# One graph layer and a top-2 mixture of experts on one core: the last four row tiles reordered, three residual sums moved from VectorE to TensorE

## The reference, cut to what matters

```
def _L0_gnn_ref(x, edge_index, W1, b1, W2, b2):        # 2500 nodes, 512 features, 80000 edges
    agg = jax.ops.segment_sum(x[src], dst, num_segments=N_NODES)
    h = jax.nn.relu((x + agg) @ W1 + b1)
    return h @ W2 + b2

def _L0_ffn_ref(x, Wg, W1, b1, W2, b2):                # 8 experts, top 2, hidden size 256
    gate = softmax(xt @ Wg);  topv, topi = top_k(gate, 2);  topv = topv / (sum(topv) + 1e-6)
    out = sum over e of (gelu(xt @ W1[e] + b1[e]) @ W2[e] + b2[e]) * scores[:, e:e+1]

x = x + _L0_gnn_ref(_layernorm(x), edge_index, ...)    # called x2 below
x = x + _L0_ffn_ref(_layernorm(x), ...)                # the second layer norm gives xt
```

## Time and profile before

| | |
|---|---|
| median of 3 runs | 658.34 us (656.91 to 659.75) |
| profiled execution, its own time | 657.24 us |
| its span in the profile | 655.5 us |
| mean granted TensorE clock | 0.946 of full speed |
| graph sums end | 412.4 us from the span's start |
| first matmul of the expert stage | 458.75 us |
| first rows added to the output | 467.98 us |
| TensorE busy | 555.8 us, 85% of the span |
| VectorE, ScalarE, GpSimd busy | 413.9, 316.7, 251.2 us |

### The profile page before, as it was taken

How to read it: one execution, slowest core, us unless ns; L and a number is a source line. 1 busy time by engine, 2 the same in 40 slices (tenths; PEclk the granted TensorE clock), 3 DMA queues, 4 the chain that set the end, 5 groups by cost and what they waited for, 6 DMA issues and landing times.

```text
span 655.5 us, 10719 instructions
## 1 busy us (share of the span) xinstructions
PE 555.8 (85%) x3842; PEld 435.9 (67%) x3843; DVE 413.9 (63%) x805; ACT 316.7 (48%) x579; POOL 251.2 (38%) x219
## 2 busy tenths in 40 slices
PE   4776877799999999999999999925999999999900
PEld 2666767656756766766666665725989998889800
DVE  5866574687369777976986131589566664554541
ACT  2573766533252125124322300558776766777671
POOL 4450222203016005100700331025567877778763
PEclk9997899999899999999999999965999999999955
DMA  8160600020020310211122113779688989899995
GB/s 259 54 161 1 192 1 1 1 75 1 1 64 2 95 48 12 84 48 49 49 77 65 39 58 96 262 236 304 139 172 183 186 167 193 187 205 198 165 185 76
DMA packets 40302, 71.91 MB, mean 110 GB/s; under 512 B 10313, under 2 KB 14545, under 8 KB 39714
## 3 DMA queue, kind: packets, MB, share of 16 engines
q0 software_dynamic: 12704, 29.22, 22.6%
q1 hardware_dynamic: 26257, 37.34, 19.3%
q10 hardware_dynamic: 1288, 4.66, 2.4%
HBM read 46.07 MB, written 26.69 MB: 111 GB/s over the span
## 4 chain that ended last, share of the span: by engine, by line
PE 50%; DMA 13%; DVE 12%; POOL 10%; ACT 7%; issue 6%; SPq 1%; ACTq 0%; POOLq 0%; DVEq 0%
PE psum L1414 26%; PE psum L1398 9%; PE psum L1451 7%; POOL out_x L601 6%; DMA out_x<-y,target_i 6%; PE psum L1330 3%; POOL xg L594 3%; DVE hot_key L1047 2%; DMA slot_rows<-edge_pairs,start_i 2%; DVE hot_lo L1047 2%; DMA xg<-xt_d,token_i 2%; DMA b_now<-in_L_ffn_b 2%; DVE xT_rest L891 1%; DVE stat L861 1%; ACT y L823 1%
## 5 line engine op out<-in xcount | busy, mean ns | idle before, releaser
L663 ACT ACTIVATE counts<-psum 128x400 bf16<-128x400 f32 x125 | 62.6, 504 | 163.2 <-PE psum L1398 162.9
L1047 DVE TENSOR_TENSOR hot_key<-iota_key,key_w 128x1200 f16<-128x1200 f16 x125 | 105.7, 845 | 47.3 <-PE psum L1398 47.3
L1414 PE MATMUL psum<-counts,z_hi 125*128 125x500 bf16 x400 | 101.8, 375 | 1.6 <-ACT h L687 1.6
L601 POOL DMA_INDIRECT out_x<-y,target_i x54 | 88.5, 1639 | 36.3 <-SPq L480 15.0
L1414 PE MATMUL psum<-counts,z_lo 125*128 125x500 bf16 x400 | 101.5, 377 | 0.0
L1398 PE MATMUL psum<-hot_key,hot_lo 128*128 128x200 f16 x750 | 84.3, 250 | 15.6 <-DVE hot_lo L1047 14.9
L1398 PEld LDWEIGHTS psum<-hot_key,hot_lo 128*128 128x128 f16 x750 | 65.2, 98 | 39.0 <-issue 18.8
L566 POOL TENSOR_TENSOR h_lo<-h,h_hi 128x500 fp32r<-128x500 f32 x16 | 23.5, 1499 | 169.5 <-ACT h_hi L694 169.5
L1047 DVE TENSOR_TENSOR hot_lo<-iota_lo,lo_w 128x768 f16<-128x768 f16 x125 | 83.5, 668 | 0.0
L1414 PEld LDWEIGHTS psum<-counts,z_lo 125*128 125x128 f16 x400 | 39.3, 98 | 45.7 <-issue 1.1
L594 POOL DMA_INDIRECT xg<-xt_d,token_i x54 | 57.4, 1063 | 31.2 <-issue 15.5
(11 more groups left out here) (252 smaller groups left out, 1149.9 us busy)
## 6 DMA issues: line engine op xcount, KB each, us to landing
w_raw<-in_L_ffn_W SPq DMA_DIRECT2D x16, 512.0 KB, 6.8
b_now<-in_L_ffn_b SPq DMA_DIRECT2D x27, 256.0 KB, 4.9
x_res<-in_x SPq DMA_DIRECT2D x20, 224.0 KB
out_x<-x SPq DMA_DIRECT2D x20, 224.0 KB
xt_d<-xt SPq DMA_DIRECT2D x20, 224.0 KB
x_in<-in_x SPq DMA_DIRECT2D x2, 1120.0 KB
W_raw<-in_L_gnn_W ACTq DMA_DIRECT2D x2, 1024.0 KB, 5.4
out_x<-in_x SPq DMA_DIRECT2D x1, 1536.0 KB, 11.7
```

Of the source, the lines that this page charges most:

```text
L601: pool.indirect_dma_start(out=out[:, :], in_=y[:, k % YB, i], in_offset=None, out_offset=bass.IndirectOffsetOnAxis(ap=target_i[:, 2 * k + ...
L663: act.activation(counts[:, it % 2, :, place:place + W], psum[:, WIN + w % 2, 0:MW].rearrange("p (w h) -> p h w", w=W), ACT.Copy).then_inc( ...
L1047: ins = dve.tensor_tensor(hot[:, w % RING].rearrange("p s (n two) -> p s n two", two=2), iota[:].rearrange("p (o n two) -> p o n two", o=1 ...
L1414: ins = mm(psum[:, AGG + c, 0:GN], half[:, t, c * 128:(c + 1) * 128], counts[0:P, g % 2, t], start=(t == 0 and n == 0), stop=(t == T - 1 a ...
```

## The change

The last group's product is cut into gate halves (264 columns) and other halves (256 columns). TensorE takes both halves of tile 0, the gate half of tile 1 between them, then the gate halves of tiles 2 and 3, then the other half of tile 1. The other halves of tiles 2 and 3 come behind the ranking matmuls. For tiles 1 to 3 the residual is added in PSUM by a product with the identity (`add_residual`), ScalarE copies the sum out and takes mean and variance by two accumulating passes (`last_rows`), VectorE makes reciprocal and shift (`last_scale`), and ScalarE normalises (`last_norm`). The logits of the four tiles are taken in one go (`last_logits`). The residual load of tile 3 is issued ahead of the stores of tile 3 of the group before. The weight copies of experts 1 to 3 move behind the last tile's normalisation. `token_part[:, :, 0]` moves from ScalarE to VectorE.

```diff
@@ sync
             for e in range(4):
                 load_expert(e)
+            sp.wait_ge(S["x2_ready"], 4 * (G - 1))
+            load_residual(G - 1, 3)
             store(G - 2, 3)
-            load_residual(G - 1, 3)
             store(G - 1, 0)
@@ scalar
+            def last_rows(q):
+                n = 4 * (G - 1) + q
+                act.wait_ge(S["mlp2_done"], n + 1)
+                act.wait_ge(x2_out[q], 64 * (G - 1))
+                step(act.activation(x2[:, q].rearrange("p (b n) -> p b n", b=2), last_out(q), ACT.Copy, accum_out=last_ln[:, q, 0:1]))
+                step(act.activation(last_ln[:, q, 1:2], last_ln[:, q, 0:1], ACT.Copy, scale=-1.0 / D))
+                step(act.activation(xt[:, q], x2[:, q], ACT.Square, bias=last_ln[:, q, 1:2], accum_out=last_ln[:, q, 2:3]))
+                act.activation(last_ln[:, q, 3:4], last_ln[:, q, 2:3], ACT.Sqrt, scale=1.0 / D, bias=eps_t[0:P, 0:1]).then_inc(S["std2_ready"], 1)
+
+            def last_norm(q):
+                n = 4 * (G - 1) + q
+                act.wait_ge(S["shift2_ready"], n - T + G + 1)
+                act.activation(xt[:, q], x2[:, q], ACT.Identity, scale=rstd2[:, n:n + 1], bias=last_ln[:, q, 4:5]).then_inc(S["xt_ready"], 1)
+
             std2(G - 2, 3)
             split_high_up(0)
-            std2(G - 1, 0)
             norm2(G - 2, 3)
             split_high_down(0)
-            std2(G - 1, 1)
+            std2(G - 1, 0)
+            last_rows(1)
             norm2(G - 1, 0)
-            split_high_up(1)
-            std2(G - 1, 2)
-            norm2(G - 1, 1)
-            split_high_down(1)
-            norm2(G - 1, 2)
-            std2(G - 1, 3)
-            split_high_up(2)
-            norm2(G - 1, 3)
-            split_high_down(2)
-
-            act.wait_ge(S["at_tile_ready"], 1)
-            act.activation(token_part[:, :, 0], at_tile[:], ACT.Copy, scale=iota_p[:]).then_inc(S["parts_ready"], 1)
-            split_high(3)
+            last_rows(2)
+            last_norm(1)
+            last_rows(3)
+            last_norm(2)
+            last_norm(3)
+            for e in range(1, 4):
+                split_high(e)
             act.wait_ge(S["shifted_ready"], 1)
@@ vector
+            def last_logits():
+                dve.wait_ge(S["gate_columns"], 2)
+                for q in range(4):
+                    n = 4 * (G - 1) + q
+                    ins = dve.tensor_tensor(logits[:, n], psum[0:P, 2 * q + 1, DH:DH + NE], gate_in[:, n], ALU.add)
+                step(ins)
+                ...
+            def last_scale(q):
+                n = 4 * (G - 1) + q
+                dve.wait_ge(S["std2_ready"], n + 1)
+                step(dve.reciprocal(rstd2[:, n:n + 1], last_ln[:, q, 3:4]))
+                dve.tensor_tensor(last_ln[:, q, 4:5], last_ln[:, q, 1:2], rstd2[:, n:n + 1], ALU.mult).then_inc(S["shift2_ready"], 1)
+
             for m in range(KC):
                 dve.wait_ge(S["h1_hi_ready"], 4 * (G - 1) + m + 1)
                 dve.tensor_tensor(last_lo[:, m], h1[:, m], last_hi[:, m].bitcast(F32), ALU.subtract).then_inc(S["h1_split"], 1)
-            logits_of(G - 2, 3)
+                if m == 2:
+                    logits_of(G - 2, 3)
             residual(G - 2, 3)
-            for q in range(3):
-                logits_of(G - 1, q)
-                residual(G - 1, q)
-                residual_end(*((G - 1, q - 1) if q else (G - 2, 3)))
-            residual_end(G - 1, 2)
-            logits_of(G - 1, 3)
+            residual(G - 1, 0)
+            residual_end(G - 2, 3)
+            residual_end(G - 1, 0)
+            last_logits()
@@ vector, routing: residual(G - 1, 3) and residual_end(G - 1, 3) are taken out;
@@ last_scale(1) stands ahead of picked, last_scale(2) ahead of dest_tile16,
@@ last_scale(3) behind at_tile, and then
+            dve.tensor_scalar(token_part[:, :, 0], at_tile[:], iota_p[:], None, ALU.mult).then_inc(S["parts_ready"], 1)
@@ tensor
+            def last_part(q, k, bank, columns):
+                rows = slice(q * P, (q + 1) * P)
+                for n, (h_, w_) in enumerate([(last_hi, W2_hi), (last_hi, W2_lo), (last_lo, W2_hi)]):
+                    ins = mm(psum[0:P, bank, 0:columns.stop - columns.start], h_[:, k, rows], w_[:, k, columns],
+                             start=(k == 0 and n == 0), stop=(k == KC - 1 and n == 2))
+                return ins
+            ...
+            def add_residual(q):
+                pe.wait_ge(S["res_sum"], 4 * (G - 1) + q + 1)
+                for b in range(2):
+                    ins = mm(psum[0:P, 2 * q + b, 0:DH], ident[0:P, 0:P], x_res[:, q, b * DH:(b + 1) * DH],
+                             start=False, stop=True, skip_group_check=True)
+                ins.then_inc(S["mlp2_done"], 1)
             mlp2(G - 2, 3)
-            for q in range(4):
-                mlp2(G - 1, q)
-
+            for k in range(KC):
+                pe.wait_ge(S["h1_split"], 4 * (G - 1) + k + 1)
+                last_gates(0, k)
+                ins = last_halves(0, k)
+                if k == 1:
+                    last_gates(1, 0)
+                if k == KC - 1:
+                    ins.then_inc(S["mlp2_done"], 1)
+                if k >= 1:
+                    last_gates(1, k)
+            for q in (2, 3):
+                if q == 3:
+                    pe.wait_ge(S["x2_ready"], 4 * (G - 1))
+                for k in range(KC):
+                    ins = last_gates(q, k)
+            ins.then_inc(S["gate_columns"], 1)
+            for k in range(KC):
+                last_halves(1, k)
+            pe.wait_ge(S["x2_ready"], 4 * (G - 1) + 1)
             pe.wait_ge(S["chosen_ready"], 1)
             pe.wait_ge(S["route_tables"], 1)
             choices = either[:].rearrange("p n e -> p (n e)")
             mm(psum[0:P, 0, 0:T * NE], before[:], choices, start=True, stop=True)
             mm(psum[0:P, 1, 0:T * NE], ones16[:], choices, start=True, stop=True).then_inc(S["ranked"], 1)
+            add_residual(1)
+            for q in (2, 3):
+                for k in range(KC):
+                    last_halves(q, k)
+                add_residual(q)
```

More of the change, by code:

```diff
@@ L104, in gnn_moe @@
         rstd2 = keep("rstd2", [P, T], F32)
+        last_ln = keep("last_ln", [P, 4, 5], F32)
         logits = keep("logits", [P, T, NE], F32)
@@ L335, in stepper, with last_out @@
             return step
+        def last_out(q):
+            return psum[0:P, 2 * q:2 * q + 2, 0:DH]
         def counted(t):
@@ L1058, in logits_of @@
                 dve.wait_ge(S["mlp2_done"], n + 1)
[L1059 to L1063, removed]
+                step(dve.tensor_tensor(logits[:, n], psum[0:P, SM + 1, DH:DH + NE], gate_in[:, n], ALU.add))
+                step(dve.max(top[:, n], logits[:, n]))
+                step(dve.max_index(topi[:, n], top[:, n], logits[:, n]))
             def residual(g, q):
                 n = 4 * g + q
-                bank = out_bank(g, q)
                 dve.wait_ge(S["mlp2_done"], n + 1)
@@ L1119, in _ @@
                             residual_end(g - back, q)
+            def last_logits():
[4 more added lines that the diff above has]
+                step(ins)
+                for n in range(4 * (G - 1), T):
+                    ins = dve.max(top[:, n], logits[:, n])
+                step(ins)
+                for n in range(4 * (G - 1), T):
+                    ins = dve.max_index(topi[:, n], top[:, n], logits[:, n])
+                step(ins)
+            def last_scale(q):
[3 more added lines that the diff above has]
+                dve.tensor_tensor(last_ln[:, q, 4:5], last_ln[:, q, 1:2], rstd2[:, n:n + 1], ALU.mult).then_inc(S["shift2_ready"], 1)
             for m in range(KC):
@@ L1166, in _ @@
                                           float(B), slot_of[:], ALU.mult, ALU.add))
+            last_scale(1)
             for c in range(2):
@@ L1183, in pair_over @@
                 return ap.rearrange("p n (o two) -> p n o two", o=1).broadcast_to([P, rows, width // 2, 2])
+            last_scale(2)
             dve.tensor_copy(dest_tile16[:], twice(dest_tile[:]))
@@ L1430, in mlp2 @@
             def mlp2(g, q):
-                last = g == G - 1
-                bank = (WIN, AGG, AGG + 2, SM)[q] if last else SM
-                if q == 0 and not last:
+                if q == 0:
                     pe.wait_ge(S["w_split"], 1)
@@ L1436, in mlp2, with last_gates, last_halves @@
                     pe.wait_ge(S["h1_split"], 4 * (g + 1))
-                if q > 0 and not last:
+                if q > 0 or g >= 1:
                     pe.wait_ge(S["x2_ready"], 4 * g + q)
-                elif q == 0 and g >= 1 and not last:
-                    pe.wait_ge(S["x2_ready"], 4 * g)
-                if last and q == 3:
-                    pe.wait_ge(S["x2_ready"], 4 * g)
                 rows = slice(q * P, (q + 1) * P)
-                hi, lo = (last_hi, last_lo) if last else (h1_hi, h1_lo)
-                trio = [(hi, W2_hi), (hi, W2_lo), (lo, W2_hi)]
```

(13 more changed lines are left out.)

16 lines of the change are left out of this document (6 added, 10 removed).

## The result

| | before | after |
|---|---|---|
| median | 658.24 us (656.91 to 659.75, 4 runs) | 672.91 us (672.61 to 675.39, 4 runs) |
| ratio | | 1.0238, 95% interval 1.0208 to 1.0269 |
| span of the profiled execution | 655.5 | 671.0 |
| mean granted clock | 0.946 | 0.935 |

The change makes the kernel 14.7 us slower. The sign was forecast, the size was not: the prediction said 663.5, with 657 to 668, and the sum behind it gave 663.9 to 666.1.

The account below looks back on a forecast made before the run. It took the late last residual load to bound the routing; 3.2 us won there is paid back in waits, and late weights delay the input 6.6 to 8.9. Added to 657.2: 663.9 to 666.1; stated 663.5, range 657 to 668.

Parts of the forecast that it names:

- 0.25 MB of residual ends at 426.3: Last residual load, queued behind experts 0 to 3, lands 3.2 us earlier than 429.5; counts then start at 431.1.
- The choice is ready at 427.9: VectorE's expert choice, the ranking's other input, ends at 427.9, so GpSimd's tables still end last.
- Identity products, the upper end for f32: TensorE's residual add: two plain f32 matmuls of 256 columns per tile, taken at 0.94 us for the pair.
- The clock: TensorE, idle before the ranking, runs at full clock or half for the first 5.9 us; VectorE's waits 1.8 or 3.9.
- `last_rows` 2.1 and `token_part` 1.0: ScalarE's `last_rows` takes 2.1 us, bounds 1.7 and 2.5; `token_part[:, :, 0]` adds 1.0 on VectorE.
- rival 4: ScalarE's square needs another activation table, two loads for each of three tiles: 7.7 us, 671; chance 0.07.
- The last xt at 441.45 to 443.65: Last normalised tile, on which the stores and later weight loads hang, ready then instead of at 436.67.
- This took 4.15 up to the first issue: SyncE's stores and their landing, from the last `xt` to the first issue of experts 5 to 7: 4.15 us.
- The gathers slow the weights, 16.1 from issue to landing: Weights of experts 5 to 7, issued at 445.6 to 447.8, meet the gathers; last piece lands at 461.6 to 463.9.
- rival 2: Weights of experts 5 to 7 keep 0.37 MB/us beside the gathers: input 1.6 to 3.9 late, 658.8 to 661.1; chance 0.25.
- A shift of the 456.9 passes 1:1: Any delay of the first block's input, at 456.9 before, reaches the end of the kernel in full.
- Rival 3: Not slower: residual load overtakes the weights, lands at 423.5, counts start at 429.0; 656.7, or 661.4 with slowed weights; chance 0.17.

Follow-up runs that it names:

- e4: Kernel before, with SyncE holding the loads of experts 5 to 7 until the block table is known: 667.38 us, ratio 1.0125 to the kernel before.
- e5: Changed kernel, with ScalarE copying the weights of experts 5 to 7 in the second to fourth block: 666.61 us, ratio 1.0134 to the kernel before.
- e13: Changed kernel, with GpSimd's gathers held until expert 7's weights have landed: 670.44 us, one run.
- e3: Changed kernel, with the last tile's residual load issued between the weights of experts 1 and 2: 665.65 us, ratio 1.0116 to the kernel before.
- e2: Changed kernel, with 84 filler matmuls in TensorE's idle time before the ranking: 671.88 us, ratio 1.0192 to the kernel before.
- e6: Changed kernel with split residual load, late copies, tile 3's scale ahead of `at_tile`, tile 1's sum and tile 2's other half before ranking: 656.42 us, ratio 0.9985 to before.
- e1: Changed kernel, with residual sums of tiles 1 and 2 and other halves of tiles 2 and 3 ahead of ranking: 667.33 us, ratio 1.0131 to the kernel before.

## Why the prediction was wrong

The mechanism was right and is shown: late weights, met by the gathers, copied by ScalarE ahead of the first block's input (e4, e5, e13). The sum gave 6.6 to 8.9 for it and the profile has 14.8 at the same place (471.67 against 456.90). Along the prediction's own steps:

- **"0.25 MB of residual ends at 426.3": the step that failed first.** It landed at 429.9, 3.6 later. The weights ahead of it, which the prediction had through at 425.6, landed at 429.5: the last piece was issued at 417.36 and took 12.1. 1.0 of the 3.6 is a graph stage that ended later in this execution (413.6). Another part is what the queue carried. The rate was the forecast one (359 to 388 GB/s from 416 to 428), but the bytes were more. From 413.6 to 430 (packets, MB, share of 16 engines):

```profile
q1 hardware_dynamic: 3653, 4.95, 87.6%
```

4.95 MB are the 4.2 of weights, the 0.26 of the load and 0.5 for the stores of tile 15, which SyncE issued behind the load, from 423.97. The sum had nothing for these. At 0.37 MB/us they are 1.4 us, an estimate; no run takes them out, and the last 1.2 of the 3.6 stay open. e3 shows the queue as the cause: with two experts fewer ahead, the load took 2.9. So the 3.2 us to be won became a loss of 0.4, and the hole on TensorE, VectorE and ScalarE lasted until 434.2.

- **The choice is ready at 427.9.** `either` ended at 428.0. Right.
- **Identity products, the upper end for f32.** Line 1488 has four records for two matmuls of 256 columns. They took 1.03 at full clock, against 0.94 in the sum, and 1.98 and 1.77 at half. Right. This agrees with the four passes of the Trainium skill, FP8 and Floating Point Precision, TensorE Precision Notes.
- **The clock.** Half for 6.1 us of the sums, the upper bound. VectorE's waits of 1.15, 2.13 and 0.64 are the 3.9 of that case. Right in size, and e2 shows the lower one (1.55 against 1.8).
- **`last_rows` 2.1 and `token_part` 1.0.** Measured 2.1 (436.50 to 438.60) and 0.80. Right. No table load stood ahead of the square, so rival 4 is out.
- **The last xt at 441.45 to 443.65.** It came at 446.8, 3.2 over the upper bound. The counts had started 3.6 late (434.72 against 431.1), so the first step's error accounts for all of it.
- **"This took 4.15 up to the first issue": mis-sized.** It took 5.6. ScalarE finishes the rows of tiles 2 and 3 within 0.7 of each other, and SyncE then issues eight transfers in a row, from 446.15 to 449.85, where before four were left.
- **The gathers slow the weights, 16.1 from issue to landing: the mechanism is right, the transfer itself was mis-sized by 1.2.** Measured 17.3. The gathers' part was 5.0 in the sum (461.6 against the 456.6 of rival 2) and is 5.0 in e13, so rival 2 is out. What was short is the transfer alone: 11.0 in the sum, 12.3 in e13. The trace of before had it: the last piece was issued at 443.85 and took 9.0, so it landed at 452.85, 12.0 behind the first issue, and not at 451.5. By that 2.1 was to spare, not 3.4.
- **"A shift of the 456.9 passes 1:1".** The first scatter moved by 16.7, since the first block's matmuls ran at half clock (5.04 against 3.14): TensorE had waited again, 465.9 to 473.5. Not in the sum. The span grew by 15.5 only, so 1.2 of the 16.7 came back later.
- **A reading.** The prediction counts three slices with a low clock around 412 to 459. The earlier trace rows has two there (6 and 5, from 426 to 459). Nothing hangs on it.

Added up: 8.9 for the upper bound, 3.2 for the late load carried through, 1.4 for the stores, 1.2 for the transfer and 0.1 for the two copies makes 14.8, as at the first block's input. These terms are read from the same trace, so that they close is no proof of the causes; the runs are. That the medians differ by as much, 14.7, is in part luck: 1.0 of the 14.8 is the later graph stage of this execution, and the 1.9 for the half clock is not in it. Rival 3, the load that overtakes the weights, is what e3 brought about by order; it alone did not bring the kernel back to before.

A part was also not asked: whether what stands behind the weights in SyncE's queue would be late. e5 and e6 showed that the bias of the first gelu was the next wait in both. The range ended at 668. Its upper end took in a bound of 0.4 a tile for ScalarE, but no bound for the landing of the load on which every later time was built. The stated 663.5 also lay below the sum's own low end of 663.9, on the hope that the gathers would leave the weights more; they did not.

## What to carry to other kernels

Before you price a reordering, find the last event that everything behind it hangs on, here one store that releases three megabytes of weights, and follow that event, not the busy engine. A transfer issued earlier into a full queue need not land earlier (here 5.0 us earlier in, 0.4 later there); put it ahead of what fills the queue, and look at what is then behind (a store, a bias of 8 KB). Work moved off a busy engine must land in time that the other engine has free: the same sums, two of three moved ahead of the ranking, gave about 7 of the 14.7 us back (e1).

## What the runs showed of the hardware

- A read of ScalarE's accumulator is an instruction of its own, 0.19 us long, behind each activation that accumulates; it overlaps by 0.1.
- A plain f32 product of 256 columns is two records: four records took 1.03 us at full clock, and 1.98 and 1.77 at half. `tensor_scalar` on 2240 f16 elements took 0.80 on VectorE, where the product of two tensors takes 1.32 and ScalarE took 2.16.
- In the changed kernel TensorE stayed at half clock for 30 us after 447 (granted clock 0.50 in each stretch of 2 us from 448 to 476), with bursts of 3.9 and (with a gap of 0.6) 6.5 us in between, and was at full again from 478. Its last product before the fall ended at 442.9.
- Six loads of 0.5 MB on SyncE's queue took 17.3 us from the first issue to the last landing beside GpSimd's gathers, and 12.3 with the gathers held (e13). The gathers' median time to landing is 6.9 in the changed kernel, 4.9 before.
